# Two of six short convolutions move from VectorE to TensorE, as products with diagonal matrices

## The chip, the core and the metric

The kernel runs on one core of one Trainium2 chip. The metric is device time in microseconds (us). A time that is compared is a median over several runs; the profile is of one execution and has its own time.

## What is computed

A gated linear attention layer with a ternary feed-forward behind it, on 8 sequences of 256 tokens with 256 channels, all in float32. The part that matters here is the projection to q, k and v with a causal convolution over four tokens for each channel, and SiLU behind it:

```python
def causal_dwconv_silu(x, w):
    """Depthwise causal conv1d (kernel CONV) + SiLU. x: [B,T,C], w: [C,K]."""
    K = w.shape[1]
    xp = jnp.pad(x, ((0, 0), (K - 1, 0), (0, 0)))
    y = jax.lax.conv_general_dilated(jnp.transpose(xp, (0, 2, 1)), w[:, None, :], (1,), 'VALID', feature_group_count=w.shape[0])
    return jax.nn.silu(jnp.transpose(y, (0, 2, 1)))
...
q = causal_dwconv_silu(x @ Wq.T, conv_wq).reshape(B, T, H, DK)
k = causal_dwconv_silu(x @ Wk.T, conv_wk).reshape(B, T, H, DK)
v = causal_dwconv_silu(x @ Wv.T, conv_wv).reshape(B, T, H, DV)
beta = jax.nn.sigmoid(x @ Wb.T)
g = -jnp.exp(A_log) * jax.nn.softplus(x @ Wa.T + dt_bias)
...
def step(S, inp):
    qt, kt, vt, gt, bt = inp
    S = S * jnp.exp(gt)[..., None, None]
    v_new = vt - jnp.einsum('bhk,bhkv->bhv', kt, S)
    S = S + bt[..., None, None] * (kt[..., :, None] * v_new[..., None, :])
    o = jnp.einsum('bhk,bhkv->bhv', qt, S)
    return (S, o)
```

There are 6 heads, with 32 channels each for q and k and 64 for v: 768 projected channels, which are six groups of 128.

## The kernel before

The eight sequences are worked in four pairs of 512 tokens. For each pair a front part makes q, k, v and small matrices for each chunk of 32 tokens, and a recurrence then carries the state over the eight chunks. The program of each engine is written by hand in the order in which it is to run, and semaphores (`after(engine, semaphore, count, ...)`) hold the engines together; no scheduler moves anything.

A **prologue** makes the front of pair 0 and, for all pairs at once, the gates beta and g. Then come four **turns**. Turn k (function `turn` of each engine) runs the recurrence of pair k through chunks c = 0 to 7, and between its steps lies the front of pair k+1, in turns 0, 1 and 2, and the tail (output projection, layer norms, feed-forward) of pair k-1.

One chunk step goes round four engines. TensorE multiplies into the bank `pc` (`from_state`, `solve`), ScalarE copies the result to `u_sb` (`u_out`, L686), TensorE multiplies it into `pc` again and then into `po` (`to_state`), VectorE adds the state `s_sb` (`next_state`, L1085), and TensorE reads it for the next chunk; VectorE makes `r_sb` on the way (`residual`, L1073), and ScalarE copies `po` out (L693).

A group j of 128 projected channels passes through these steps:

- `project(k, j)`, L346: TensorE makes the group's projection in one half of the bank pair `pj`, half j mod 2, from two float32 products of 512 columns.
- `tile_out_of_psum(k, j)`: ScalarE copies it to `raw` (L623), a tile with three zero columns ahead of each sequence, and writes it, times the last tap, to the tile `conv`, which the profile calls `conv_buf` (L624).
- `conv_taps(k, j)`, L928: VectorE adds the other three taps, one instruction for each.
- `silu(k, j)`, L650: ScalarE takes SiLU into `kq` (groups 0 to 2) or `v_ch`, the tile named `x1_buf` in the program and `x_buf` in the profile (groups 3 to 5). Groups 2 and 5 take four instructions on 64 partitions each.

Behind the six groups, in chunks 3 and 4 of a turn, come `exponents` (L367, TensorE, into both halves of `pj`) with `exp_d` (L656, ScalarE), `square` (L664, ScalarE), `v_to_tokens` (L949, VectorE), `factors` (from L962, VectorE), and the matrices `dt_m` and `cm` on GpSimd (L849, L854).

In the prologue ScalarE's order is: the copies and SiLUs of all six groups, then `alog` (L802) and the softplus of the gates (L804 to L807), which waits for VectorE's preparation of `abt`. TensorE's order is: six projections, then 32 narrow products for the gates (L572), then a product that spreads the gates over the partitions (L579), which waits for VectorE.

## Time and profile before

| | us |
|---|---|
| median of 3 runs | 422.68 (421.88 to 423.92) |
| the profiled execution, its own time | 424.54 |
| its span, first to last instruction | 422.7 |
| VectorE busy | 315.2 (75%) |
| TensorE busy, products | 268.4 (63%) |
| ScalarE busy | 142.2 (34%) |
| GpSimd busy | 45.8 (11%) |
| mean granted TensorE clock | 0.766 of full |

No engine is busy all the time. The span is a chain that goes from engine to engine, so what counts is which work the chain passes through, and the order in which each engine takes its work. Times below are from the span's start. Turn 0 begins at about 82 us, turn 1 at about 158, turn 2 at about 250 and turn 3 at about 339.

### The profile page before, as it was taken

What the parts mean: (1) busy time and instruction counts of PE and PEld (TensorE: products, weight loads), DVE (VectorE), ACT (ScalarE), POOL (GpSimd) and SP (SyncE); (2) the same over time, 40 slices, a digit from 0 to 9 for tenths busy, and PEclk for the clock granted to TensorE, in tenths of its full rate; (3) what the DMA queues carried; (4) which work ended last, traced back from release to release, by engine and by line L of the source; (5) the groups of instructions that cost most, each with busy time, mean ns of one, the idle gap of its engine ahead of it and who ended that gap; (6) DMA issues with size and microseconds to landing.
All of it is one profiled execution on the core that took longest, in us unless ns stands there. A gap on an engine that the chain in (4) does not pass through costs nothing.

```text
span 422.7 us, 14141 instructions
## 1 busy us (share of the span) xinstructions
PE 268.4 (63%) x6314; PEld 181.3 (43%) x6314; DVE 315.2 (75%) x790; ACT 142.2 (34%) x341; POOL 45.8 (11%) x59
## 2 busy tenths in 40 slices
PE   3992710598576639797586559785666093986552
PEld 1481500545454417364554436454534072754431
DVE  0765998938698993949698996767989938248996
ACT  0874540047704610354523412357036000232010
POOL 1000240002520000012320000025200000000000
PEclk9965675589867867988666679897888567899665
DMA  8400000000000010000000020000000111000101
GB/s 255 181 0 2 2 0 0 5 2 3 4 3 2 4 50 3 2 3 2 3 4 2 3 99 3 2 4 2 5 2 2 51 51 53 3 3 14 40 0 50
DMA packets 8012, 9.70 MB, mean 23 GB/s; under 512 B 1808, under 2 KB 7056, under 8 KB 7952
## 3 DMA queue, kind: packets, MB, share of 16 engines
q1 hardware_dynamic: 7024, 8.41, 6.0%
q8 instruction: 49, 0.80, 0.8%
q10 hardware_dynamic: 928, 0.39, 0.4%
q14 instruction: 11, 0.09, 0.1%
HBM read 6.70 MB, written 2.10 MB: 21 GB/s over the span
## 4 chain that ended last, share of the span: by engine, by line
DVE 53%; PE 30%; issue 7%; ACT 6%; DMA 1%; DVEq 0%; SPq 0%; ACTq 0%
PE pc L333 7%; PE pj L346 6%; PE pg L457 4%; DVE sub_buf L1027 3%; DVE conv_buf L928 3%; DVE sub_buf L1025 3%; PE fr L572 2%; PE fr L480 2%; PE pj L457 2%; PE fr L333 2%; DVE chunk_buf L984 2%; DVE r_sb L1073 2%; DVE ss L962 2%; DVE r_all L916 1%; DVE t_all L915 1%
## 5 line engine op out<-in xcount | busy, mean ns | idle before, releaser
L928 DVE SCALAR_TENSOR_TENSOR conv_buf<-raw,wconv,conv_buf 128x512 f32<-128x512 f32 x72 | 55.5, 777 | 16.5 <-ACT conv_buf L624 14.8
L346 PE MATMUL pj<-xt,wproj 128*128 128x512 f32 x96 | 54.6, 705 | 8.2 <-DMA xt<-x_t 7.3
L686 ACT ACTIVATE u_sb<-pc 128x192 f32<-128x192 f32 x32 | 10.5, 329 | 116.3 <-PE pc L333 116.2
L876 POOL TENSOR_TENSOR s_dec<-s_sb,decay 128x192 f32<-128x192 f32 x24 | 14.5, 602 | 264.2 <-DVE s_sb L1082 169.6
L333 PE MATMUL pc<-r_sb,t_t 32*32 32x64 f32 x672 | 17.8, 244 | 35.2 <-DVE r_sb L1073 34.5
L333 PEld LDWEIGHTS pc<-r_sb,t_t 32*32 32x32 f32 x672 | 12.6, 120 | 46.0 <-DVE r_sb L1073 42.8
L333 PE MATMUL fr<-dt_m,chunk_buf 32*32 32x32 f32 x768 | 10.5, 219 | 34.3 <-DVE dt_m L1041 20.2
L346 PEld LDWEIGHTS pj<-xt,wproj 128*128 128x128 f32 x96 | 19.4, 221 | 26.9 <-issue 22.6
L358 PE MATMUL pg<-xt,wproj 128*128 128x512 f32 x48 | 29.6, 747 | 0.0
L457 PE MATMUL pg<-wout,conv_buf 128*128 128x256 f32 x36 | 15.2, 607 | 19.5 <-DVE conv_buf L1119 19.5
L333 PEld LDWEIGHTS fr<-dt_m,chunk_buf 32*32 32x32 f32 x768 | 9.7, 131 | 35.9 <-issue 35.9
L333 PE MATMUL pc<-u_sb,kg_tok 32*32 32x64 f32 x672 | 17.8, 246 | 11.3 <-ACT u_sb L686 11.3
L723 ACT ACTIVATE rv<-v_tok,bv 128x64 f32<-128x64 f32 x96 | 23.9, 338 | 0.0
L333 PEld LDWEIGHTS pc<-u_sb,kg_tok 32*32 32x32 f32 x672 | 12.7, 122 | 24.6 <-ACT u_sb L686 14.0
L693 ACT ACTIVATE o_all<-po 128x192 f32<-128x192 f32 x32 | 10.5, 329 | 33.8 <-PE po L333 33.7
L333 PE MATMUL pc<-s_sb,kc_ch 32*32 32x64 f32 x672 | 16.8, 236 | 7.8 <-DVE s_sb L1085 4.4
L457 PEld LDWEIGHTS pg<-wout,conv_buf 128*128 128x128 f32 x36 | 11.0, 315 | 24.8 <-DVE conv_buf L1119 22.4
L1085 DVE TENSOR_TENSOR s_sb<-s_dec,pc 128x192 f32<-128x192 f32 x24 | 8.4, 348 | 17.0 <-PE pc L333 16.8
L333 PE MATMUL po<-u_sb,a_t 32*32 32x64 f32 x768 | 19.3, 238 | 1.8 <-ACT u_sb L686 1.8
L333 PEld LDWEIGHTS pc<-s_sb,kc_ch 32*32 32x32 f32 x672 | 12.2, 116 | 17.0 <-issue 9.7
L333 PE MATMUL fr<-kq 32*32 32x64 f32 x768 | 19.0, 273 | 0.0
L333 PEld LDWEIGHTS fr<-kq 32*32 32x32 f32 x768 | 17.4, 146 | 1.2 <-issue 1.1
(161 smaller groups left out, 577.4 us busy)
## 6 DMA issues: line engine op xcount, KB each, us to landing
xt<-x_t SPq DMA_DIRECT2D x1, 1536.0 KB, 9.1
x_buf<-x SPq DMA_DIRECT2D x3, 512.0 KB, 3.8
out<-hid_buf SPq DMA_DIRECT2D x6, 256.0 KB, 2.2
wproj<-w_proj SPq DMA_DIRECT2D x1, 1024.0 KB, 8.1
xt<-x_t SPq DMA_DIRECT2D x1, 512.0 KB, 5.9
kq<-x SPq DMA_DIRECT2D x1, 512.0 KB, 3.7
out<-v_tok SPq DMA_DIRECT2D x2, 256.0 KB, 2.1
wout<-w_out SPq DMA_DIRECT2D x1, 384.0 KB, 9.5
```

Source lines behind the costliest of these rows:

```text
L333: mm = pe.matmul(out[rows], stationary[rows], moving[rows], **flags)
L346: mm = pe.matmul(pj[:, j % 2, :], wproj[:, t, j * P:(j + 1) * P], xt[:, t, k * TOK:(k + 1) * TOK], start=(t == 0), stop=(t == KT - 1))
L358: mm = pe.matmul(pg[:, :], wproj[:, t, w * P:(w + 1) * P], xt[:, t, k * TOK:(k + 1) * TOK], start=(t == 0), stop=(t == KT - 1))
L457: mm = pe.matmul(y_bank[part][:, (n % 2) * HID:(n % 2 + 1) * HID], o_ch[:, j, n * P:(n + 1) * P], wout[:, j, :], start=(j == 0), stop=(j = ...
L480: mm = pe.matmul(fr[:, n // 2, (n % 2) * HID:(n % 2 + 1) * HID], xq_t[:, n, t, :], wsplit[:, w, t, :], start=(t == 0 and w == 0), stop=(t ...
L686: act.activation(u_sb[:, :, :].rearrange("p g v -> p (g v)"), pc[:, 0:G3 * DV], ACT.Copy).then_inc(u_done, 1)
L693: act.activation(o_all[:, :, c, :], po[:, 0:G3 * DV].rearrange("p (g v) -> p g v", g=G3), ACT.Copy).then_inc(o_out, 1)
L723: e = act.activation(rv[:, k % 2, g, c, :], v_tok[:, g, c, :, :].rearrange("p h v -> p (h v)"), ACT.Identity, scale=bv[:, g * NC + c:g * N ...
L876: pool.tensor_tensor(s_dec[:, :, :], s_sb[:, :, :], decay[:, :, c:c + 1].to_broadcast([P, G3, DV]), ALU.mult).then_inc(sdec_done, 1)
L928: e = dve.scalar_tensor_tensor(out=conv[:, d, :, :], in0=raw[:, d, :, m:m + T], scalar=wconv[:, j, m:m + 1], in1=conv[:, d, :, :], op0=ALU ...
L1025: own(dve.tensor_tensor(step, inv16[:, j:j + 1, :, j + 1:HALF].to_broadcast(grid), inv16[:, 0:j, :, j:j + 1].to_broadcast(grid), ALU.mult))
L1027: own(dve.tensor_tensor(below, below, step, ALU.add))
```

## The change

Groups 4 and 5 (`BANK_TILES`) are no longer convolved by VectorE. At the start VectorE builds eight diagonal matrices `wdiag` of 128 x 128, one for each tap of each of the two groups. ScalarE copies the projection to `raw` as before but writes no `conv` tile for these groups. TensorE then multiplies the four shifted views of `raw` by the four diagonal matrices, float32 by float32 and 512 columns each, and adds them up in the same half of `pj` from which `raw` was copied (`conv_in_bank`). ScalarE takes SiLU straight from there.

```diff
+BANK_TILES = (4, 5)
+COPIED_TILES = CONV_TILES - len(BANK_TILES)
...
+        wdiag = sb("wdiag", [P, len(BANK_TILES), TAPS, P])
...
+            def conv_in_bank(k, j):
+
+                n = BANK_TILES.index(j)
+                if first(k):
+                    pe.wait_ge(diag_done, len(BANK_TILES) * TAPS)
+                after(pe, raw_in, n + 1, k, len(BANK_TILES))
+                for m in range(TAPS):
+                    mm = pe.matmul(pj[:, j % 2, :], wdiag[:, n, m, :], raw[:, SLOT[j], :, m:m + T],
+                                   start=(m == 0), stop=(m == TAPS - 1))
+                mm.then_inc(conv_mm, 1)
...
             def exponents(k):
 
                 after(pe, gm_done, 1, k, 1)
-                after(pe, tile_out, CONV_TILES, k, CONV_TILES)
+                after(pe, silu_done, CONV_TILES, k, CONV_TILES)
...
                     if front and c == 3:
-                        exponents(k + 1)
+                        conv_in_bank(k + 1, 4)
                     if front and c == 4:
                         chunk_products(k + 1, 0)
                     to_state(k, c)
+                    if front and c == 3:
+                        conv_in_bank(k + 1, 5)
+                    if front and c == 4:
+                        exponents(k + 1)
                     if front and c == 4:
                         chunk_products(k + 1, 1)
...
             mm.then_inc(ab_done, 1)
             pe.wait_ge(ld_const, 16)
+            for j in BANK_TILES:
+                conv_in_bank(0, j)
             pe.wait_ge(rep_in, 4)
...
-                act.activation(raw[:, SLOT[j], :, TAPS - 1:], bank, ACT.Copy)
+                moved = act.activation(raw[:, SLOT[j], :, TAPS - 1:], bank, ACT.Copy)
+                if j in BANK_TILES:
+                    moved.then_inc(raw_in, 1)
+                    return
...
             def silu(k, j):
-                after(act, conv_done[j], 1, k, 1)
+                if j in BANK_TILES:
+                    after(act, conv_mm, BANK_TILES.index(j) + 1, k, len(BANK_TILES))
+                    conved = pj[:, j % 2, :].rearrange("p (b t) -> p b t", b=2)
+                else:
+                    after(act, conv_done[j], 1, k, 1)
+                    conved = conv[:, SLOT[j], :, :]
...
-                    if front and c == 3:
-                        silu(k + 1, 4)
                     o_out_of_psum(k, c)
...
                     if front and c == 3:
+                        silu(k + 1, 4)
+                        silu(k + 1, 5)
+                    if front and c == 4:
                         exp_d(k + 1)
-                        silu(k + 1, 5)
...
-                    if front and c == 3:
-                        conv_taps(k + 1, 4)
...
-                    if front and c == 3:
-                        conv_taps(k + 1, 5)
...
             dve.wait_ge(ld_conv, 16)
-            for j in (0, 1):
-                conv_taps(0, j)
-            for j in range(2, CONV_TILES):
+            dve.wait_ge(ld_const, 16)
+            for n, j in enumerate(BANK_TILES):
+                for m in range(TAPS):
+                    dve.tensor_scalar(wdiag[:, n, m, :], cst[:, C_IDENT:C_IDENT + P], wconv[:, j, m:m + 1],
+                                      None, ALU.mult).then_inc(diag_done, 1)
+            for j in range(COPIED_TILES):
                 conv_taps(0, j)
```

Three places show what stands in a row on an engine before and now. Each row is an instruction or several equal ones, with the semaphores that it waits for. Lines of the changed program carry other numbers: L679 there is L650 here, L831 and L833 are L802 and L804, L715 is L686, L722 is L693, L685 is L656, L693 is L664, L337 is L333 and L382 is L367; L361 is `conv_in_bank`.

First ScalarE in the prologue, from the SiLU of group 3 to the first step of the softplus, before:

```order
L650 ACTIVATE x_buf<-conv_buf 128x2x256 [waits conv_done3]
L650 ACTIVATE x_buf<-conv_buf 128x2x256 [waits conv_done4]
L650 ACTIVATE x_buf<-conv_buf 64x256 [waits conv_done5]
L650 ACTIVATE x_buf<-conv_buf 64x256 x3
L802 ACT_TABLE_LOAD
L802 ACTIVATE alog<-alog 128x6 [waits ld_small]
L804 ACTIVATE abt<-abt 128x16x6 [waits abt_abs]
```

and after the change:

```order
L679 ACTIVATE x_buf<-conv_buf 128x2x256 [waits conv_done3]
L679 ACTIVATE x_buf<-pj 128x2x256 [waits conv_mm]
L679 ACTIVATE x_buf<-pj 64x256 [waits conv_mm]
L679 ACTIVATE x_buf<-pj 64x256 x3
L831 ACT_TABLE_LOAD
L831 ACTIVATE alog<-alog 128x6 [waits ld_small]
L833 ACTIVATE abt<-abt 128x16x6 [waits abt_abs]
```

The SiLUs of groups 4 and 5 keep their places ahead of `alog` and the softplus, and what they wait for is now TensorE's `conv_mm`.

Second TensorE in turn 0, from the solve of chunk 3 to the solve of chunk 4, before:

```order
L333 MATMUL pc<-r_sb,t_t 32x64 x11
L367 MATMUL pj<-gm,cst 128x384 [waits tile_out,gm_done]
L367 MATMUL pj<-gm,cst 128x384
L333 MATMUL pc<-u_sb,kg_tok 32x64 [waits u_done]
L333 MATMUL pc<-u_sb,kg_tok 32x64 x11
L333 MATMUL po<-u_sb,a_t 32x64 x12
L333 MATMUL pc<-s_sb,kc_ch 32x64 [waits s_done]
L333 MATMUL pc<-s_sb,kc_ch 32x64 x11
L333 MATMUL po<-s_sb,qe_ch 32x64 [waits o_out]
L333 MATMUL po<-s_sb,qe_ch 32x64 x11
L333 MATMUL pc<-r_sb,t_t 32x64 [waits r_done]
L333 MATMUL pc<-r_sb,t_t 32x64 x11
```

and after the change, as far as the products that open chunk 4:

```order
L337 MATMUL pc<-r_sb,t_t 32x64 x11
L361 MATMUL pj<-raw,wdiag 128x512 [waits raw_in]
L361 MATMUL pj<-raw,wdiag 128x512 x3
L337 MATMUL pc<-u_sb,kg_tok 32x64 [waits u_done]
L337 MATMUL pc<-u_sb,kg_tok 32x64 x11
L337 MATMUL po<-u_sb,a_t 32x64 x12
L361 MATMUL pj<-raw,wdiag 128x512 [waits raw_in]
L361 MATMUL pj<-raw,wdiag 128x512 x3
L337 MATMUL pc<-s_sb,kc_ch 32x64 [waits s_done]
L337 MATMUL pc<-s_sb,kc_ch 32x64 x11
L337 MATMUL po<-s_sb,qe_ch 32x64 [waits o_out]
L337 MATMUL po<-s_sb,qe_ch 32x64 x11
```

The convolution of group 4 stands between the solve of chunk 3 and its state product, that of group 5 between the state product and the start of chunk 4, and the exponents are no longer here: the diff has them behind the state product of chunk 4.

Third ScalarE in chunks 3 and 4 of turn 0, before:

```order
L686 ACTIVATE u_sb<-pc 128x192 [waits u_mm]
L650 ACTIVATE x_buf<-conv_buf 128x2x256 [waits v_tok_done,conv_done4]
L693 ACTIVATE o_all<-po 128x3x64 [waits o_mm]
L656 ACT_TABLE_LOAD
L656 ACTIVATE gm<-pj 128x384 [waits dexp_mm]
L656 ACTIVATE gm<-pj 128x384
L650 ACT_TABLE_LOAD [waits v_tok_done]
L650 ACTIVATE x_buf<-conv_buf 64x256 [waits conv_done5]
L650 ACTIVATE x_buf<-conv_buf 64x256 x3
L664 ACTIVATE gate_buf<-tok_buf 128x1536 [waits og_done,kq_tok_done]
L686 ACTIVATE u_sb<-pc 128x192 [waits u_mm]
L693 ACTIVATE o_all<-po 128x3x64 [waits o_mm]
```

and after the change:

```order
L715 ACTIVATE u_sb<-pc 128x192 [waits u_mm]
L722 ACTIVATE o_all<-po 128x3x64 [waits o_mm]
L679 ACTIVATE x_buf<-pj 128x2x256 [waits v_tok_done,conv_mm]
L679 ACTIVATE x_buf<-pj 64x256 [waits v_tok_done,conv_mm]
L679 ACTIVATE x_buf<-pj 64x256 x3
L693 ACTIVATE gate_buf<-tok_buf 128x1536 [waits og_done,kq_tok_done]
L715 ACTIVATE u_sb<-pc 128x192 [waits u_mm]
L722 ACTIVATE o_all<-po 128x3x64 [waits o_mm]
L685 ACT_TABLE_LOAD
L685 ACTIVATE gm<-pj 128x384 [waits dexp_mm]
L685 ACTIVATE gm<-pj 128x384
```

Both SiLUs now stand behind the copy of `po` in chunk 3, with the square and the `u_sb` copy of chunk 4 behind them; the exponentials and their table load stand behind chunk 4's copy of `po`, and the load that brought SiLU back is gone from here.

## Rows read from the trace of the kernel before

**Rows 1.** The page's chain that ended last: shares of the span by engine.

```profile
...
DVE 53%; PE 30%; issue 7%; ACT 6%; DMA 1%; DVEq 0%; SPq 0%; ACTq 0%
...
```

**Rows 2.** Groups by line: count, then busy us, mean ns, idle us before them.

```profile
...
L928 DVE SCALAR_TENSOR_TENSOR conv_buf<-raw,wconv,conv_buf 128x512 f32<-128x512 f32 x72 | 55.5, 777 | 16.5 <-ACT conv_buf L624 14.8
...
L624 ACT ACTIVATE conv_buf<-pj,wconv 128x512 f32<-128x512 f32 x24 | 16.5, 687 | 0.0
...
```

**Rows 3.** Timeline of ScalarE in the prologue: start, duration, engine, line, operation, [idle before].

```profile
...
26.95 1.69 ACT L650 ACTIVATE x_buf<-conv_buf 64x256 f32<-64x256 f32 x4 [0.96 <-DVE conv_buf L928]
28.66 1.28 ACT L802 ACT_TABLE_LOAD   x1
29.95 0.21 ACT L802 ACTIVATE alog<-alog 128x6 f32<-128x6 f32 x1
32.00 0.29 ACT L804 ACTIVATE abt<-abt 128x96 f32<-128x96 f32 x1 [1.84 <-DVE abt L1328]
...
```

**Rows 4.** Timeline of VectorE in the prologue.

```profile
...
13.40 13.52 DVE L928 SCALAR_TENSOR_TENSOR conv_buf<-raw,wconv,conv_buf 128x512 f32<-128x512 f32 x18 [13.40 <-ACT conv_buf L624]
30.78 0.36 DVE L1324 COPY ab<-fr 128x192 f32<-128x192 f32 x1 [3.86 <-PE fr L572]
...
```

**Rows 5.** Transfers: issuing queue, count, size, us to landing.

```profile
...
cst<-consts ACTq DMA_DIRECT2D x1, 371.5 KB, 6.0
...
```

**Rows 6.** Timeline of TensorE: float32 products at full clock, and bfloat16 ones.

```profile
...
13.33 7.13 PE L346 MATMUL pj<-xt,wproj 128*128 128x512 f32 x16 [0.91 <-ACT conv_buf L624]
...
95.01 1.98 PE L346 MATMUL pj<-xt,wproj 128*128 128x512 f32 x4
...
187.80 1.48 PE L480 MATMUL fr<-wsplit,tok_buf 128*128 128x256 bf16 x12
...
```

**Rows 7.** Chain of waits in order of time: four half-clock records.

```profile
...
85.73 3.44 PE pj L346 x4
...
```

**Rows 8.** Busy time by stretch; behind the fifth engine PEclk, the granted clock.

```profile
...
28.00:30.00 2.00, 2.00 (x11) 2.00 (x11) 0.00 (x0) 1.96 (x4) 0.00 (x0) 0.50 0.00 0
...
```

**Rows 9.** Timeline of TensorE in chunks 3 and 4, turns 0, 1 and 2.

```profile
...
104.75 1.56 PE L367 MATMUL pj<-gm,cst 128*128 128x384 f32 x4
...
114.48 0.86 PE L333 MATMUL pc<-u_sb,kg_tok 32*32 32x64 f32 x24 [2.92 <-ACT u_sb L686]
...
195.27 2.89 PE L367 MATMUL pj<-gm,cst 128*128 128x384 f32 x4
198.10 0.54 PE L333 MATMUL pc<-u_sb,kg_tok 32*32 32x64 f32 x24
198.46 0.51 PE L333 MATMUL po<-u_sb,a_t 32*32 32x64 f32 x24
...
285.15 1.56 PE L367 MATMUL pj<-gm,cst 128*128 128x384 f32 x4
...
```

**Rows 10.** Timeline of ScalarE in chunks 3 and 4, turns 0, 1 and 2.

```profile
...
111.00 1.69 ACT L650 ACTIVATE x_buf<-conv_buf 64x256 f32<-64x256 f32 x4
112.72 1.48 ACT L664 ACTIVATE gate_buf<-tok_buf 128x1536 f32<-128x1536 f32 x1
114.11 0.31 ACT L686 ACTIVATE u_sb<-pc 128x192 f32<-128x192 f32 x1
...
205.97 0.31 ACT L686 ACTIVATE u_sb<-pc 128x192 f32<-128x192 f32 x1
...
219.96 0.60 ACT L703 ACTIVATE gate_buf<-pg 128x512 f32<-128x512 f32 x1 [3.77 <-PE pg L358]
...
294.92 0.31 ACT L686 ACTIVATE u_sb<-pc 128x192 f32<-128x192 f32 x1
...
```

**Rows 11.** Timeline of VectorE in turns 0 and 1, behind the state of chunk 4.

```profile
...
115.68 1.74 DVE L962 TENSOR_REDUCE ss<-gate_buf 128x48 f32<-128x1536 f32 x1
...
218.24 0.96 DVE L999 STREAM_TRANSPOSE chunk_buf<-dt_m 128x768 f32<-128x768 f32 x1
...
```

**Rows 12.** Timeline of GpSimd in turn 1: the mask over the exponentials.

```profile
...
202.72 1.80 POOL L849 TENSOR_TENSOR dt_m<-gm,cst 128x768 f32<-128x768 f32 x1
...
```

More of the change, by code:

```diff
@@ L228, in program @@
         zeroed, vec_own, act_own, ffn_ready = (sem(n) for n in ("zeroed", "vec_own", "act_own", "ffn_ready"))
+        diag_done, raw_in, conv_mm = (sem(n) for n in ("diag_done", "raw_in", "conv_mm"))
         proj_done, tile_out, silu_done, kc_part, on_scaled = (
@@ L342, in project @@
                         after(pe, y_in, 0, k - 1, 2)
-                if not (first(k) and j < 2):
-                    after(pe, tile_out, j - 1, k, CONV_TILES)
+                if j >= 2:
+                    after(pe, tile_out, j - 1, k, COPIED_TILES)
                 for t in range(KT):
@@ L649, in silu @@
                     src = slice(0, 2) if b is None else b
-                    e = act.activation(dst, conv[rows, SLOT[j], src, :], ACT.Silu)
+                    e = act.activation(dst, conved[rows, src, :], ACT.Silu)
                 e.then_inc(silu_done, 1)
@@ L924, in conv_taps @@
             def conv_taps(k, j):
-                after(dve, tile_out, j + 1, k, CONV_TILES)
+                after(dve, tile_out, j + 1, k, COPIED_TILES)
                 for m in range(TAPS - 1):
```

## The prediction

> **What bounds the kernel now.** I read the page first, then the groups by line, then the chain of waits and the timelines of the two places that the change touches. The chain that ended last runs over VectorE for 53% of the span and over TensorE for 30% [rows 1], so VectorE instructions look like what it pays to remove, and the convolution's are the costliest group: 72 of 777 ns [rows 2]. But the diff takes only those of groups 4 and 5, at fixed places, so the question is which wait ends last at those places: once in the prologue, and in chunks 3 and 4 of turns 0, 1 and 2.
>
> In the prologue VectorE sits idle for 3.86 us behind the convolutions, until 30.78, when TensorE's gate products (L572) are done [rows 4]. ScalarE is idle for 1.84 us ahead of the softplus step L804, which starts at 32.00 [rows 3]. From there the path goes through softplus, gates and chunk matrices with no long idle time; the end of the six groups has slack and L804 has none.
>
> In chunks 3 and 4 the step that holds the recurrence is ScalarE's `u_sb` copy of chunk 4 (114.11, 205.97, 294.92). It stands straight behind the SiLU of group 5 and the square, and once it is done TensorE goes on after 2.92 us of idleness [rows 9, 10]. VectorE's reduction L962 follows at 115.68 [rows 11]; from there to the chunk matrices VectorE is nearly full, so a delay of this copy is passed on to the end.
>
> **The price of one convolution.** It is four float32 products of 512 columns, against two for a projection, so eight records of the kind of L346. Sixteen such records at full clock take 7.13 us and four take 1.98 us [rows 6]. Both fit r = 0.43 us a record plus 0.26 us at the end. At half clock four take 3.44 us [rows 7], 0.86 each. The next TensorE work starts 0.06 to 0.07 us before such a group's recorded end (195.27 + 2.89 against 198.10) [rows 9], ScalarE 0.04 after it. So a convolution at 2.4 GHz costs TensorE 8 x 0.43 + 0.19 = 3.63 us, and ScalarE may read it after 8 x 0.43 + 0.30 = 3.74 us. Reading through shifted views of `raw` and a diagonal stationary matrix have no row of their own; I take the projection's rate, since type, columns and partitions are the same. The lower bound is the bfloat16 row: 12 records of 256 columns in 1.48 us [rows 6], which is about 0.21 us for 512 columns, half of r.
>
> The Trainium skill ("TensorE: Matmul & The Clock Gate", section "Back-to-back issue gap") gives about 131 ns a pass for sustained streams of 512 columns, against 216 ns alone. By that a record of two passes would be 0.26 us instead of 0.43 and the whole change would come to about +3 us. The trace speaks for the slower figure: 16 records in a row keep 0.43 us [rows 6].
>
> **Prologue.** TensorE's two convolutions stand behind the gate products, so they start at 30.7. The granted clock there is 0.50 of full, that is 1.2 GHz [rows 8]: 32 narrow products have not kept it up. How many of the 16 records stay at half clock is not shown. Elsewhere four did (3.44 us) [rows 7], or the 2.83 us of the exponents from 195.27 before the rows turned short [rows 9]. I take four: 3.44 + 12 x 0.43 = 8.60 us, and 0.30 more until ScalarE starts the SiLU of group 5, at 39.60. All at full clock would be 6.88, all at half 13.76.
>
> ScalarE works in order, and both SiLUs stand ahead of `alog` and the softplus. Behind the SiLU of group 5 come its own 1.71 us (26.95 to 28.66), the table load to 29.95 (1.29), and `alog`, 0.23 [rows 3]. So L804 starts at 39.60 + 3.23 = 42.83 instead of 32.00: **+10.83 us**, 9.1 if all records run at full clock and 16.0 if none does. VectorE waits for the softplus and everything behind waits for VectorE; I find nothing later there that has been waiting for something else.
>
> The Trainium skill ("ScalarE: Activation LUTs", section "What ACT_TABLE_LOAD costs") adds a drain of about 1.38 us to each load. That would make it +12.2. The trace shows none: the load starts 0.02 us after the SiLU and `alog` 0.01 us after the load [rows 3].
>
> What VectorE loses there, 6 instructions of some 0.75 us, lies ahead of 3.86 us of idleness and gains nothing. The eight diagonals are built before 13.40, where VectorE has nothing else [rows 4]; the constants take 6.0 us to land [rows 5]. Even at 0.78 us each (a full convolution tap, four times as wide) they would end at about 13.5, so they cost nothing. ScalarE's two spared `conv` writes of 0.69 us [rows 2] gain nothing for the same reason.
>
> **Chunks 3 and 4 of a turn.** Let E be the start of the exponents today: 104.75, 195.27, 285.15 [rows 9]. The convolution of group 4 starts there instead, its `raw` being there since chunk 2. Then follow in TensorE's order the state product of chunk 3, 0.80 us (198.10 to 198.46 + 0.51, less the 0.07), and the convolution of group 5. ScalarE then does the SiLU of group 5 and the square, 3.11 us from its start to that of the `u_sb` copy (111.00 to 114.11) [rows 10]. Sum: 3.63 + 0.80 + 3.74 + 3.11 = 11.28 us behind E. In turn 1 the exponents ran at half clock, 2.89 us against 1.56; three records of the first convolution there are 0.43 us longer, +1.29.
>
> - turn 0: 104.75 + 11.28 = 116.03 against 114.11, +1.92
> - turn 1: 195.27 + 12.57 = 207.84 against 205.97, +1.87
> - turn 2: 285.15 + 11.28 = 296.43 against 294.92, +1.51
>
> TensorE has no long gap ahead of chunk 4's state product any more, so I take that at 0.54 us instead of 0.86 [rows 9] and subtract 0.32 from each: +1.60, +1.55, +1.19, **+4.3 us** together. Of what goes away (VectorE's six instructions, the exponents ahead of the state product, exponentials and table loads between two `u_sb` copies) all is counted, since E + 11.28 holds none of it.
>
> Moved work that is hidden: VectorE's layer-norm moments in chunk 3 now run while TensorE convolves. The exponents run behind chunk 4's state product, the exp load beside them, then the exponentials and GpSimd's mask, 1.80 us [rows 12]. In turn 1 that ends at about 215, and the matrices (L999, today 218.24) want it at about 220 [rows 11]. The SiLU table returns ahead of the gate's SiLU, where ScalarE is idle for 3.77 us [rows 10] against a load of 1.28. If that cover were gone each would cost its own length, at most 1.3 us a turn.
>
> **Sum.** 10.8 + 4.3 = +15.2 us. The profiled execution, 424.54, becomes 439.7; it lies 1.86 above the median, so the median 422.68 becomes **437.9 us**.
>
> **Rivals.**
>
> *Not slower, cheap products.* As a function of r the prologue gives 20r + 2.2 and the turns 51r - 17.6, together 71r - 15.4. It is zero at r = 0.216. If products with `raw` ran at the bfloat16 row's 0.213 us a record, the two convolutions would hide where VectorE's did and the time would be 422.4. Only the bfloat16 row speaks for it; every float32 row of 512 columns speaks against. Chance 0.03. A gain beyond 0.5% needs r under 0.19, which no row shows.
>
> *The turns break even.* The recurrence may get the 4.3 us back: at full clock the later solve and state products, as the one of 0.86 us [rows 9], would be 0.32 shorter, and two or three a turn lie on the path; a wait later in the turn may also end on something else. Then only the prologue counts: 422.68 + 10.8 = 433.5. For it: TensorE is busier. Against: VectorE is the fuller engine after 115.68 [rows 11]. Chance 0.14.
>
> *The clock stays low.* All 16 records of the prologue at half clock are +5.2, and one more first convolution of a turn at half clock is +3.4: 437.9 + 8.6 = 446.5. For it: rows at 0.50 in the prologue [rows 8]; against: dense work of this kind has brought the clock back in each row I read. Chance 0.11.
>
> **Chances and range.** Forecast 0.72. About 0.5%, some 2 us, is what a measurement of this kernel can tell from no change. Faster by more than that 0.01, within it 0.03, slower 0.96. The lower end takes the break-even turns and the prologue at full clock partly (9.1 + 1 is 432.8), the upper the prologue wholly at half clock (443.1): **432.5 to 443.5 us**.
>
> **What would show it.** In the changed profile: ScalarE idle for some 10 us ahead of the SiLU of group 4 in the prologue and some 3 us ahead of that of group 5, released by TensorE's L361; the `alog` table load at about 41.3; eight convolution records in 3.7 us in each turn; chunk 4's `u_sb` copy 11.3 us behind the first of them; VectorE idle in chunk 3 where its taps stood. I am wrong if L361's records are far from 0.43 us, if the softplus doesn't wait for them, or if the stretch from chunk 5 to the next turn changes its length by more than 1 us.

## The result

| | before | changed |
|---|---|---|
| median, us | 423.24 (421.88 to 423.92, 4 runs) | 441.91 (439.73 to 443.68, 4 runs) |
| the profiled execution, own time | 424.54 | 441.51 |
| its span | 422.7 | 439.7 |
| mean granted TensorE clock | 0.766 | 0.800 |

The changed kernel is slower: ratio (its time over that of before) 1.0443, 95% interval 1.0387 to 1.0499. The forecast was 437.9 us with a range of 432.5 to 443.5. The page of the changed kernel, busy times and the chain by engine:

```profile
PE 292.2 (66%) x6378; PEld 188.7 (43%) x6378; DVE 303.2 (69%) x774; ACT 136.5 (31%) x333; POOL 42.0 (10%) x59
...
DVE 49%; PE 37%; issue 6%; ACT 5%; DMA 1%; DVEq 0%; SPq 0%; ACTq 0%
```

VectorE was relieved of 12 us and TensorE was given 24, and the chain moved the same way: 37% over TensorE now, where [rows 1] had 30%. The groups by line (count, busy us, mean ns, idle us before them), where [rows 2] had 72 taps:

```profile
L957 DVE SCALAR_TENSOR_TENSOR conv_buf<-raw,wconv,conv_buf 128x512 f32<-128x512 f32 x48 | 36.6, 769 | 7.1 <-ACT conv_buf L648 6.0
L361 PE MATMUL pj<-raw,wdiag 128*128 128x512 f32 x64 | 31.9, 646 | 0.0
```

So 18.9 us of VectorE's taps became 31.9 us of TensorE's products. Line numbers have moved: L928 is L957 now, L650 is L679, L664 is L693, L686 is L715, L804 is L833, L849 is L878, L962 is L991.

**The prologue** of the changed kernel, TensorE (start, duration, engine, line, operation, [idle before]), then ScalarE. These answer to [rows 3, 6]:

```profile
27.80 2.50 PE L591 MATMUL fr<-wab,xt 128*128 128x12 f32 x11
30.14 9.71 PE L361 MATMUL pj<-raw,wdiag 128*128 128x512 f32 x16
```

```profile
36.46 0.60 ACT L679 ACTIVATE x_buf<-pj 128x512 f32<-128x512 f32 x1 [11.76 <-PE pj L361]
39.89 1.55 ACT L679 ACTIVATE x_buf<-pj 64x256 f32<-64x256 f32 x4 [2.84 <-PE pj L361]
41.46 1.28 ACT L831 ACT_TABLE_LOAD   x1
42.75 0.21 ACT L831 ACTIVATE alog<-alog 128x6 f32<-128x6 f32 x1
42.87 0.27 ACT L833 ACTIVATE abt<-abt 128x96 f32<-128x96 f32 x1
```

ScalarE does nothing for 11.76 and then 2.84 us, each time released by TensorE's L361, with the softplus step L833 behind it in its order. That step starts at 42.87; it was at 32.00.

**Chunks 3 and 4 of turn 0** of the changed kernel: TensorE, then ScalarE, against [rows 9, 10]:

```profile
116.03 3.70 PE L361 MATMUL pj<-raw,wdiag 128*128 128x512 f32 x8
119.67 0.54 PE L337 MATMUL pc<-u_sb,kg_tok 32*32 32x64 f32 x24
120.03 0.51 PE L337 MATMUL po<-u_sb,a_t 32*32 32x64 f32 x24
120.47 3.70 PE L361 MATMUL pj<-raw,wdiag 128*128 128x512 f32 x8
...
127.67 0.54 PE L337 MATMUL pc<-u_sb,kg_tok 32*32 32x64 f32 x24 [1.12 <-ACT u_sb L715]
```

```profile
120.83 0.59 ACT L679 ACTIVATE x_buf<-pj 128x512 f32<-128x512 f32 x1
124.21 1.55 ACT L679 ACTIVATE x_buf<-pj 64x256 f32<-64x256 f32 x4 [2.78 <-PE pj L361]
125.78 1.49 ACT L693 ACTIVATE gate_buf<-tok_buf 128x1536 f32<-128x1536 f32 x1
127.29 0.33 ACT L715 ACTIVATE u_sb<-pc 128x192 f32<-128x192 f32 x1
```

The `u_sb` copy of chunk 4 starts 127.29 - 116.03 = 11.26 us behind the first convolution. Eight records take 3.70 us and the next TensorE work starts 3.64 us in.

**Behind the reduction `ss`** come VectorE's small factors, with GpSimd's mask beside them, both of the changed kernel in turn 0.

```profile
130.97 0.18 DVE L943 TENSOR_TENSOR rt<-r 128x24 f32<-128x24 f32 x1
131.18 0.18 DVE L944 SCALAR_TENSOR_TENSOR rt<-rt,kk 128x24 f32<-128x24 f32 x1
131.40 1.67 DVE L945 SCALAR_TENSOR_TENSOR r<-rt,r 128x24 f32<-128x24 f32 x1
133.11 0.18 DVE L943 TENSOR_TENSOR rt<-r 128x24 f32<-128x24 f32 x1
```

```profile
131.20 1.83 POOL L878 TENSOR_TENSOR dt_m<-gm,cst 128x768 f32<-128x768 f32 x1 [8.27 <-ACT gm L685]
```

L945 on 24 elements a partition takes 0.18 us each time but one in a turn: when it starts 0.20 us behind the mask it is over at 133.07, 0.04 us after the mask's end. The same stands at 223.15 and 315.15. In the kernel before, the mask ran at 110.81 in turn 0, while VectorE had nothing to do.

**Where the 17.0 us of the two profiled executions lie.** The marks are VectorE's reduction `ss` (the first is the prologue's) and its reduction `m_o`, which opens the tail; the interval columns are differences of their starts in the two traces.

| interval | before | changed | difference | predicted |
|---|---|---|---|---|
| start to first `ss` | 45.89 | 56.97 | +11.08 | +10.83 |
| to `ss` in turn 0 | 69.79 | 71.58 | +1.79 | +1.60 |
| to `m_o` | 30.53 | 32.00 | +1.47 | 0 |
| to `ss` in turn 1 | 61.33 | 59.75 | -1.58 | +1.55 |
| to `m_o` | 30.53 | 31.71 | +1.18 | 0 |
| to `ss` in turn 2 | 58.42 | 60.29 | +1.87 | +1.19 |
| to `m_o` | 30.55 | 31.71 | +1.16 | 0 |
| to the end | 95.7 | 95.7 | 0.0 | 0 |

Prologue +11.1, convolutions in the turns +2.1, the stretches behind `ss` +3.8. The prediction named a change of more than 1 us from chunk 5 to the next turn as a sign of being wrong; that is the interval from `ss` to `m_o`, and it changed by 1.2 to 1.5 us in each turn.

### The profile page after: what moved, and what is told of

Read it like the earlier page. It is cut to its first block, busy times and chain, and to the rows that moved or that the text cites. A ratio compares the mean times of both kernels' runs of the same rounds, so it can differ in the third digit from the quotient of the medians.

```text
span 439.7 us, 14243 instructions
## 1 busy us (share of the span) xinstructions
PE 292.2 (66%) x6378; PEld 188.7 (43%) x6378; DVE 303.2 (69%) x774; ACT 136.5 (31%) x333; POOL 42.0 (10%) x59
## 2 busy tenths in 40 slices
DMA packets 8013, 9.71 MB, mean 22 GB/s; under 512 B 1808, under 2 KB 7056, under 8 KB 7952
## 4 chain that ended last, share of the span: by engine, by line
DVE 49%; PE 37%; issue 6%; ACT 5%; DMA 1%; DVEq 0%; SPq 0%; ACTq 0%
PE pc L337 8%; PE pj L361 7%; PE pj L350 6%; PE pg L472 3%; DVE sub_buf L1056 3%; DVE sub_buf L1054 3%; PE fr L337 3%; PE fr L591 2%; PE fr L495 2%; PE pj L472 2%; DVE r_sb L1102 2%; DVE conv_buf L957 2%; DVE ss L991 2%; DVE r L945 2%; PE po L337 1%
## 5 line engine op out<-in xcount | busy, mean ns | idle before, releaser
L715 ACT ACTIVATE u_sb<-pc 128x192 f32<-128x192 f32 x32 | 10.6, 331 | 111.3 <-PE pc L337 111.2
L957 DVE SCALAR_TENSOR_TENSOR conv_buf<-raw,wconv,conv_buf 128x512 f32<-128x512 f32 x48 | 36.6, 769 | 7.1 <-ACT conv_buf L648 6.0
L905 POOL TENSOR_TENSOR s_dec<-s_sb,decay 128x192 f32<-128x192 f32 x24 | 13.1, 547 | 266.2 <-DVE s_sb L1111 167.4
L337 PE MATMUL pc<-r_sb,t_t 32*32 32x64 f32 x672 | 17.3, 241 | 30.7 <-DVE r_sb L1102 29.4
L337 PE MATMUL fr<-dt_m,chunk_buf 32*32 32x32 f32 x768 | 12.0, 237 | 37.3 <-DVE dt_m L1070 20.0
L361 PE MATMUL pj<-raw,wdiag 128*128 128x512 f32 x64 | 31.9, 646 | 0.0
L337 PEld LDWEIGHTS pc<-r_sb,t_t 32*32 32x32 f32 x672 | 12.2, 118 | 41.2 <-DVE r_sb L1102 40.6
L337 PEld LDWEIGHTS fr<-dt_m,chunk_buf 32*32 32x32 f32 x768 | 11.2, 151 | 38.9 <-issue 38.9
L373 PE MATMUL pg<-xt,wproj 128*128 128x512 f32 x48 | 26.2, 671 | 0.0
L472 PE MATMUL pg<-wout,conv_buf 128*128 128x256 f32 x36 | 14.0, 565 | 18.0 <-DVE conv_buf L1148 18.0
L1102 DVE TENSOR_TENSOR r_sb<-pc,rv 128x192 f32<-128x192 f32 x28 | 9.9, 352 | 22.8 <-PE pc L337 22.4
L722 ACT ACTIVATE o_all<-po 128x192 f32<-128x192 f32 x32 | 10.5, 329 | 44.4 <-PE po L337 44.4
L337 PE MATMUL pc<-u_sb,kg_tok 32*32 32x64 f32 x672 | 17.3, 241 | 8.3 <-ACT u_sb L715 8.3
L337 PEld LDWEIGHTS pc<-u_sb,kg_tok 32*32 32x32 f32 x672 | 12.2, 118 | 21.1 <-ACT u_sb L715 10.9
L337 PE MATMUL po<-u_sb,a_t 32*32 32x64 f32 x768 | 19.4, 235 | 2.5 <-ACT u_sb L715 1.8
L337 PE MATMUL pc<-s_sb,kc_ch 32*32 32x64 f32 x672 | 16.6, 234 | 4.5 <-DVE s_sb L1114 2.0
L361 PEld LDWEIGHTS pj<-raw,wdiag 128*128 128x128 f32 x64 | 12.5, 204 | 14.3 <-issue 13.7
```

The source lines that it names most:

```text
L337: mm = pe.matmul(out[rows], stationary[rows], moving[rows], **flags)
L361: mm = pe.matmul(pj[:, j % 2, :], wdiag[:, n, m, :], raw[:, SLOT[j], :, m:m + T], start=(m == 0), stop=(m == TAPS - 1))
L373: mm = pe.matmul(pg[:, :], wproj[:, t, w * P:(w + 1) * P], xt[:, t, k * TOK:(k + 1) * TOK], start=(t == 0), stop=(t == KT - 1))
L472: mm = pe.matmul(y_bank[part][:, (n % 2) * HID:(n % 2 + 1) * HID], o_ch[:, j, n * P:(n + 1) * P], wout[:, j, :], start=(j == 0), stop=(j = ...
L715: act.activation(u_sb[:, :, :].rearrange("p g v -> p (g v)"), pc[:, 0:G3 * DV], ACT.Copy).then_inc(u_done, 1)
L905: pool.tensor_tensor(s_dec[:, :, :], s_sb[:, :, :], decay[:, :, c:c + 1].to_broadcast([P, G3, DV]), ALU.mult).then_inc(sdec_done, 1)
```

## The experiments

The theory was: the prologue costs some 10.8 us because the softplus stands behind the two SiLUs, the turns some 4 because two convolutions and the square stand in a row ahead of `u_sb`, and, as the trace of the changed kernel added, the mask costs VectorE 1.5 us a turn. The rivals: more products cost everywhere (a slower clock, a busier TensorE), or the parts hide behind each other.

The kernel before was measured again beside each set of runs, at 423.9, 424.5 and 424.2 us, so a difference of 1 us between runs of two sets says nothing.

### Softplus first

```diff
-            for j in range(CONV_TILES - CONV_DEPTH, CONV_TILES):
+            for j in range(CONV_TILES - CONV_DEPTH, COPIED_TILES):
                 silu(0, j)
...
             act.activation(abt[:, :, H:2 * H], ab[:, :, H:2 * H], ACT.Tanh, scale=0.5).then_inc(soft_done, 1)
+            for j in BANK_TILES:
+                silu(0, j)
```

> Only ScalarE's order in the prologue differs from the changed kernel: the softplus of the gates stands ahead of the SiLUs of groups 4 and 5. Theory (the prologue's price is the softplus queued behind the SiLUs that wait for TensorE): the softplus step starts near 32 us again instead of 42.87; TensorE's spreading product still can't start before the second convolution ends, at about 39.8 instead of 37.6, but then runs at full clock and is 1.3 shorter, so some 1 us stays: about 441.9 - 10.9 + 1 = 432. Rival (TensorE's own 9.7 us in the prologue are the price, whoever waits for them): no more than 2 us come back, 440 or more.

Measured: 434.02 us (432.93 to 436.33), ratio 1.0245 (1.0210 to 1.0281). The order of ScalarE alone gives 7.9 of the 18.7 us back. ScalarE in this run's prologue:

```profile
33.03 0.29 ACT L833 ACTIVATE abt<-abt 128x96 f32<-128x96 f32 x1 [6.94 <-DVE abt L1358]
...
41.39 1.54 ACT L679 ACTIVATE x_buf<-pj 64x256 f32<-64x256 f32 x4 [2.84 <-PE pj L361]
...
45.64 1.49 ACT L693 ACTIVATE gate_buf<-tok_buf 128x1536 f32<-128x1536 f32 x1
47.14 1.28 ACT L848 ACT_TABLE_LOAD   x1
```

The softplus is back at 33.03, released by VectorE as before. The first `ss` comes at 49.38, against 56.97 in the changed kernel and 45.89 before: it now stands behind the second convolution's SiLU (2.84 us of idleness), the copies and the square behind it, and a table load (L848) that only this order needs there. The expectation had counted 1 us for what stays. Of the 3.5 us that stay in this trace, 1.28 are the load, which I had overlooked; ScalarE's copies ahead of the square start 2.45 us later than before (42.96 against 40.51), behind that SiLU, so part of the convolutions' length stays on the path.

### The turns alone, and the prologue alone

For the first, pair 0 keeps VectorE's convolutions and the diagonals come in from turn 0 on:

```diff
+        def banked(k, j):
+            return k > 0 and j in BANK_TILES
...
-            for j in BANK_TILES:
-                conv_in_bank(0, j)
...
-            for j in range(COPIED_TILES):
+            for j in range(CONV_TILES):
                 conv_taps(0, j)
```

> Pair 0 is convolved by VectorE as before the change, pairs 1 to 3 by TensorE as in the changed kernel. If prologue and turns are separate prices, the prologue's 10.9 us go and what is left against before is the turns: 441.9 - 10.9 = 431.0, 7 to 8 us above before; by the sum of the prediction it would be 4.3 above before, 427.5. Rival (the prologue's delay hides part of the turns' cost or the other way): more than 2 us away from 431.

Measured: 431.67 us (430.84 to 433.72), ratio 1.0191 (1.0150 to 1.0233). The trace is of the slowest of the four runs, and 2.4 us of its excess lie ahead of the first `ss` (48.26 against 45.89), though pair 0 is convolved as before: the first projection started 0.9 us later, and the gate products took 11.26 us against 10.37 (granted clock 0.62 against 0.67). The intervals behind the first `ss` add up to +6.8 us. L949, which is L945 here, takes 1.67 us again, at 123.13.

For the second, only pair 0 has the diagonals, and the turns have the order of before:

```diff
+        def banked(k, j):
+            return k == 0 and j in BANK_TILES
...
                     if front and c == 3:
-                        conv_in_bank(k + 1, 4)
+                        exponents(k + 1)
...
-                    if front and c == 3:
-                        conv_in_bank(k + 1, 5)
-                    if front and c == 4:
-                        exponents(k + 1)
```

> The other half: only pair 0 is convolved by TensorE, and the turns are those of before. Theory: 423.2 + 10.9 = 434.1. Rival (later work absorbs part of the prologue's delay): under 432.

Measured: 435.08 us (434.66 to 435.32), ratio 1.0264 (1.0235 to 1.0293). The softplus starts at 42.22 and the first `ss` at 56.02. In its trace all intervals behind the first `ss` together are as before, within 0.1 us. The product of the two ratios is 1.0460; the whole change has 1.0443, well within its interval. So the parts add as far as can be measured. By the medians the 18.7 us are 11 in the prologue and 8 in the turns; by the traces the turns cost 6 to 7.

### Most of the mask left out

```diff
-                pool.tensor_tensor(dt_m[:, :, :], dexp[:, :, :], upper, ALU.mult).then_inc(dt_done, 1)
+                n = U if first(k) else 1
+                pool.tensor_tensor(dt_m[:, 0:n, :], dexp[:, 0:n, :], upper[:, 0:n, :], ALU.mult).then_inc(dt_done, 1)
```

> The changed kernel, with GpSimd's mask over the exponentials of pairs 1 to 3 reading one unit of 24 and leaving the others out. Theory (the mask now runs beside VectorE's factors and blocks a small instruction with two SBUF inputs for 1.5 us in each of three turns): that instruction is 0.18 us again, and the time falls by 4.5 us to about 437.4. Rival (the slow instruction comes from something else, such as waiting for its own result, or the gap closes on another wait): 441 or more.

Measured: 438.91 us (438.38 to 439.62), ratio 1.0356 (1.0325 to 1.0387). GpSimd's mask and VectorE's L946 (L945 of the changed kernel) in turn 0:

```profile
130.44 0.28 POOL L879 TENSOR_TENSOR dt_m<-gm,cst 128x32 f32<-128x32 f32 x1 [8.26 <-ACT gm L685]
130.64 0.18 DVE L946 SCALAR_TENSOR_TENSOR r<-rt,r 128x24 f32<-128x24 f32 x1
```

L946 is short again, and `ss` to `m_o` in turn 0 takes 30.05 us, less than the 30.53 of before. Of the 4.5 us that three such waits are, 3.0 came back in the median. By the two traces the stretches behind `ss` gave back 4.3 us, and those ahead of `ss` in turns 1 and 2 took 1.9 more: the output projection ran at a lower clock there, 5.22 and 5.49 us against 4.42 and 4.74 in the changed kernel. TensorE does just as much here as in the changed kernel, so a busier TensorE doesn't explain the stretch.

### The mask later

```diff
                 after(pool, dexp_done, 1, k, 1)
+                if not first(k):
+                    after(pool, c2_done, 1, k, 1)
                 pool.tensor_tensor(dt_m[:, :, :], dexp[:, :, :], upper, ALU.mult).then_inc(dt_done, 1)
```

> The changed kernel with GpSimd's mask (dt_m) of turns 0 to 2 held back until VectorE has made c2, so that it runs beside VectorE's scaled operands and no longer beside the small factor L945 (a two-operand instruction of 0.18 us that took 1.67 us in the changed kernel). Shared-port theory (a VectorE instruction that reads two operands from SBUF waits until the GpSimd mask is over): L945 returns to 0.18 us, and the wait moves with the mask to the first scaled operand L1015, which gets some 1.5 us longer; the time stays at 441.9, within 1.5 us. Rival (L945 is long for a reason of its own, for example because what it reads has just been written by ScalarE or TensorE is busier): L945 stays at 1.67 us wherever the mask is, and the time goes up by up to 1.5 us a turn.

Measured: 442.70 us (441.25 to 444.19), ratio 1.0425 (1.0399 to 1.0450): no difference from the changed kernel. VectorE, then GpSimd, in turn 0:

```profile
131.71 0.18 DVE L947 SCALAR_TENSOR_TENSOR r<-rt,r 128x24 f32<-128x24 f32 x1
...
134.15 1.71 DVE L1015 TENSOR_TENSOR chunk_buf<-tok_buf,nceg 128x256 f32<-128x256 f32 x1
135.78 1.70 DVE L1017 TENSOR_TENSOR sub_buf<-tok_buf,park 128x256 f32<-128x256 f32 x1
137.40 0.73 DVE L1015 TENSOR_TENSOR chunk_buf<-tok_buf,nceg 128x256 f32<-128x256 f32 x1
```

```profile
133.77 1.80 POOL L880 TENSOR_TENSOR dt_m<-gm,cst 128x768 f32<-128x768 f32 x1 [10.53 <-DVE c L1002]
135.66 1.54 POOL L885 TENSOR_TENSOR gm<-c,cst 128x768 f32<-128x768 f32 x1
```

The factor (L947 here) is at 0.18 us, and the wait has gone where the mask went: the first scaled operand waits for the mask, the second for the mask over `c` behind it (in the changed kernel they took 1.38 and 0.73). The wait belongs to two instructions that run at one time, not to L945. This decides against the rival.

### Two taps instead of four

```diff
-                for m in range(TAPS):
+                for m in range(2, TAPS):
                     mm = pe.matmul(pj[:, j % 2, :], wdiag[:, n, m, :], raw[:, SLOT[j], :, m:m + T],
-                                   start=(m == 0), stop=(m == TAPS - 1))
+                                   start=(m == 2), stop=(m == TAPS - 1))
```

> The changed kernel with only two of the four diagonal products for each of groups 4 and 5; the other two taps are left out, so its output isn't the reference's. It halves the one quantity r that both terms of the prediction hang on. If every record of L361 is on the path at 0.43 us: 8 records fewer in the prologue (3.44 us) and 8 fewer in each of three turns (10.3 us), 13.8 us in all: 441.9 becomes 428.1. Rival (something else ends last in the turns once the products are short, the square or VectorE): only the prologue's 3.4 and part of the turns' come back, 434 or more.

Measured: 429.43 us (425.57 to 429.68), ratio 1.0097 (1.0059 to 1.0134): 12.5 us less than the changed kernel, 13.8 expected; the spans differ by 13.9 (439.7 against 425.8). By the traces the first `ss` came 3.3 us earlier (53.64), and each interval that ends at `ss` in a turn was 3.6 us shorter (67.96 against 71.58 in turn 0), the rest unchanged within 0.3. Eight records of 0.43 us are 3.44. So the records that were left out had lain on the path in all four places, at their full length; no second wait lies right behind.

### The square earlier

```diff
-                    if front and c == 4:
-                        square(k + 1)
...
                         silu(k + 1, 4)
+                        square(k + 1)
                         silu(k + 1, 5)
```

> The changed kernel with the square put ahead of the SiLU of group 5 on ScalarE, where ScalarE waits 2.8 us for TensorE's second convolution; 1.4 us of work leave the stretch between that convolution and the u_sb copy of chunk 4. Theory: the u_sb copy of chunk 4 starts 1.1 to 1.5 us earlier in turns 0 to 2, but VectorE's transpose of v, which waits for the SiLU of group 5, and the reduction behind it then bound the turn, so only some 0.7 us a turn reach the end: about 439.9. Rival (the u_sb copy alone carries the path): 1.4 us a turn, 437.7. Rival (the path lies on VectorE wholly): 441.9.

Measured: 439.02 us (437.48 to 439.55), ratio 1.0332 (1.0312 to 1.0352), 2.9 us less. ScalarE in turn 0, where the convolutions start at 115.80:

```profile
121.08 1.49 ACT L693 ACTIVATE gate_buf<-tok_buf 128x1536 f32<-128x1536 f32 x1
123.98 1.55 ACT L679 ACTIVATE x_buf<-pj 64x256 f32<-64x256 f32 x4 [1.41 <-PE pj L361]
125.55 0.33 ACT L715 ACTIVATE u_sb<-pc 128x192 f32<-128x192 f32 x1
```

`u_sb` stands 9.75 us behind the first convolution, 1.51 less, but `ss` only 11.76 behind it, 0.76 less: VectorE's transpose of `v_tok`, which starts with the `u_sb` copy and lasts 1.84 us, comes ahead of it. Half of the gain goes there, as the theory had it. The medians can't tell the theory (2.0 us) from the rival (4.2): they differ by 2.9 us, and the two ratios by 4.7. The traces can: `ss` gained 0.76, 0.33 and 0.76 us on the first convolution in the three turns, and the whole span 2.0 (437.7 against 439.7).

The wait beside the mask is still there, but in turns 0 and 2 it is another instruction's:

```profile
129.75 1.73 DVE L939 TENSOR_SCALAR r<-rt 128x24 int32<-128x24 int32 x1
```

```profile
129.65 1.80 POOL L877 TENSOR_TENSOR dt_m<-gm,cst 128x768 f32<-128x768 f32 x1 [6.94 <-ACT gm L685]
```

L939 reads one tile, not two, and elsewhere takes 0.18 us. So "two operands from SBUF", as the shared-port theory puts it, doesn't cover every instruction that waits.

### The other mask later, in the kernel before

The same kind of wait was already in the kernel before: its mask over `c` (L854) stands beside L984 and L986. This holds it back until `kc` is made, and moves nothing else:

```diff
                 after(pool, c2_done, 1, k, 1)
+                if not first(k):
+                    after(pool, kc_done, 1, k, 1)
                 pool.tensor_tensor(cm[:, :, :], units(c2[:, :]), lower, ALU.mult).then_inc(cm_done, 1)
...
                         d_masked(k + 1)
+                    if front and c == 5:
                         c_masked(k + 1)
```

> The kernel before with only one of the two moves of the run that gave 418.4: GpSimd's mask cm held back until VectorE has made kc. Shared-port theory: L984 takes 0.41 us instead of 1.38 and L986 0.41 instead of 0.73 in each of turns 0 to 2, 1.3 us a turn on the path: 424.5 becomes 420.6, and the square has the other 2.2 us. Rival (the whole gain came from the square): 424.

Measured: 418.71 us (417.00 to 420.92) beside 424.20 for the kernel before, ratio 0.9874 (0.9839 to 0.9910). The kernel before, turn 0, VectorE and GpSimd:

```profile
120.97 1.38 DVE L984 TENSOR_TENSOR chunk_buf<-tok_buf,nceg 128x256 f32<-128x256 f32 x1
122.27 0.73 DVE L986 TENSOR_TENSOR sub_buf<-tok_buf,park 128x256 f32<-128x256 f32 x1
```

```profile
120.59 1.48 POOL L854 TENSOR_TENSOR gm<-c,cst 128x768 f32<-128x768 f32 x1 [7.97 <-DVE c L971]
```

and with the mask later (lines moved by 3):

```profile
121.09 0.41 DVE L987 TENSOR_TENSOR chunk_buf<-tok_buf,nceg 128x256 f32<-128x256 f32 x1
121.42 0.42 DVE L989 TENSOR_TENSOR sub_buf<-tok_buf,park 128x256 f32<-128x256 f32 x1
...
124.12 0.94 DVE L996 STREAM_TRANSPOSE qe_ch<-sub_buf 128x768 f32<-128x768 f32 x1
```

```profile
124.36 1.48 POOL L856 TENSOR_TENSOR gm<-c,cst 128x768 f32<-128x768 f32 x1 [7.90 <-DVE kc_ch L994]
```

From `ss` to the transpose into `kc_ch` it is 7.43 us instead of 8.70, as expected; `ss` to `m_o` is shorter by 1.59, 1.91 and 1.92 us. The 0.3 beyond the 1.3 in turn 0 is idleness ahead of the next state (1.02 us before `s_sb` has become 0.68). The mask now runs beside the transpose L996, which takes 0.94 us as it did before without a mask beside it (125.28, L993): it did not wait.

With the square moved ahead of the copy of `po` as well:

```diff
                         silu(k + 1, 4)
+                        square(k + 1)
                     o_out_of_psum(k, c)
```

> The kernel before, not the changed one, with two moves that the study's traces point to: the square of ScalarE ahead of the copy of po and the exponentials of chunk 3 instead of ahead of the u_sb copy of chunk 4, and GpSimd's mask cm held back until VectorE has made kc, so that it does not stand beside VectorE's two-operand instructions L984 and L986. Shared-port theory: L984 and L986 lose the 1.3 us a turn that they wait (-3.9), the square 0.8 us a turn (-2.4): 423.4 becomes 417 to 418. Rival (the waits hide behind something else): 422 to 423.5.

Measured: 418.38 us (416.60 to 420.68) beside 424.46, ratio 0.9852 (0.9827 to 0.9877). It is the fastest kernel of the study, faster than both that the case began with. The two intervals overlap, so the square's share, expected at 2.4 us, can't be told from nothing. Counted from the first `ss`, `u_sb` came 0.3 us earlier in turn 0 (113.24 - 45.30 against 114.11 - 45.89) and `ss` 0.2 later (69.95 against 69.79), for the same transpose is in the way. The mask has the gain, and I had expected it at 3.9 us where it is 5.5.

### All three in the changed kernel

Softplus first, the square early and the mask over `c` late, by the edits above.

> The changed kernel with everything that the study found to give back: the SiLUs of groups 4 and 5 of pair 0 behind the gates' softplus (gave 7.9 us alone), the square ahead of the SiLU of group 5 (gave 2.9 alone), and GpSimd's mask cm held back until VectorE has made kc, away from L1013 and L1015. If the shares add: 441.9 less 7.9, 2.9 and 3.9 is 427.2. That still lies some 9 us above the kernel before with its two moves (418.4), which is the price of the convolutions on TensorE in the turns and of the L945 wait. Rival (the three moves overlap on one wait): 430 or more.

Measured: 429.40 us (427.00 to 431.35) beside 424.20, ratio 1.0113 (1.0078 to 1.0148). By the traces the stretch behind `ss` is shorter by 1.5, 1.4 and 1.3 us. It is 2.2 us above the expected 427.2. The profiled execution was the slowest of the six (431.35), and in it 1.4 us of the excess show in turn 2, TensorE:

```profile
289.77 0.74 PE L337 MATMUL pc<-r_sb,t_t 32*32 32x64 f32 x24 [0.78 <-DVE r_sb L1106]
...
290.44 5.14 PE L361 MATMUL pj<-raw,wdiag 128*128 128x512 f32 x8
...
296.32 3.70 PE L361 MATMUL pj<-raw,wdiag 128*128 128x512 f32 x8
```

The same eight records take 5.14 and 3.70 us. Busy times of 290.40 to 292.40, PEclk behind the fifth engine, show 1.2 GHz:

```profile
290.40:292.40 2.00, 2.00 (x8) 0.92 (x4) 1.18 (x7) 0.33 (x1) 0.00 (x0) 0.50 0.00 0
```

So even mended, the convolutions on TensorE cost 429.4 - 418.4 = 11 us against the kernel before with the same mask move and a like move of the square. The waits beside the mask over the exponentials are among them (in turn 0 one of 1.73 us where 0.18 is usual), and so is the prologue's first `ss`, 4.4 us later (49.74 against 45.30).

## Why the prediction came out as it did

**The price of a convolution: right.** 3.70 us for eight records, 3.64 until TensorE's next work and 3.74 until ScalarE's SiLU (120.47 to 124.21), against a forecast of 3.70, 3.63 and 3.74. Shifted views of `raw` and a diagonal stationary matrix cost what the projection's operands cost. Halving the number of products showed that each record is paid in full. The rival of cheap products is out.

The Trainium skill ("TensorE: Matmul & The Clock Gate", section "Back-to-back issue gap") gives two rates for a matmul of 512 columns. As an estimate for a record, twice its 216 ns for an isolated one is what these records show (0.43 us); twice its 131 ns for a sustained stream would have made eight records 2.1 us, where the trace has 3.70.

**The prologue: the mechanism right, the close number by errors that cancel.** L833 at 42.87, forecast 42.83. The products started 0.56 us earlier than I said (30.14). They took 9.71 us where the forecast comes to 8.86 (8.60 and the 0.26 at the end), because the clock stayed low longer: by these lengths about six records at half clock, not four. From the SiLU of group 5 to L833 it was 2.98 us, not 3.23. That is -0.56 + 0.85 - 0.25. Busy times of the changed kernel by stretch, PEclk behind the fifth engine:

```profile
32.00:34.00 2.00, 2.00 (x4) 0.97 (x3) 1.28 (x1) 0.00 (x0) 0.00 (x0) 0.50 0.00 0
34.00:36.00 2.00, 2.00 (x4) 0.73 (x4) 0.00 (x0) 0.00 (x0) 0.00 (x0) 0.65 0.00 0
36.00:38.00 2.00, 2.00 (x6) 0.79 (x6) 0.00 (x0) 0.60 (x1) 0.00 (x0) 1.00 0.00 0
```

That the order of ScalarE makes it a cost was shown by putting the softplus first. L831's table load starts 0.02 us after the SiLU (39.89 + 1.55 to 41.46). The eight diagonals cost nothing, as forecast: VectorE built them in 1.66 us from 7.49 and was then idle for 4.56 us.

The Trainium skill ("ScalarE: Activation LUTs", section "What ACT_TABLE_LOAD costs") would have a drain of 1.38 us beside that load; the trace has none.

**The convolutions in the turns: the mechanism right, the size half.** 11.26 us from the first record to `u_sb` in each of the three turns, forecast 11.28. Of +4.3 us only +2.1 came, and the difference is the clock of TensorE at other places than I had put it. In turn 1 the 1.29 us for records at half clock did not come (3.70 us at 207.78). The output projection earlier in that turn ran at a better clock, 4.42 us against 5.49 before, and so did a group's projection between it and the convolutions, 2.69 us (194.30) against 3.38 (180.59). In turn 2 it went the other way: the output projection took 4.74 us against 4.27 and the projection behind it 2.85 (286.14) against 2.60 (271.75), which is the 0.7 us by which that turn lies above its forecast. The 1.29 us were real but not where I put them. In the run with the softplus first the convolution of turn 1 took 5.04 us, in the mended changed kernel that of turn 2 took 5.14. The price belongs into the range, at no fixed place.

**"Moved work that is hidden": wrong.** This is the step of the prediction that failed. I moved GpSimd's mask to about 131 in turn 0 and asked only when its result is wanted. The result was early enough. What I left out is what VectorE does in those 1.8 us, and whether the two can run together. Those instructions can't: 1.49 us a turn in L945, 3.8 us in the three intervals behind `ss`. Leaving most of the mask out, and moving it, showed that the overlap is the cause.

The Trainium skill ("SBUF — State Buffer", section "Who interferes with whom") has the rule: a VectorE instruction with two SBUF inputs contends with a GpSimd instruction that reads SBUF, and whoever comes first keeps the shared ports for its whole length. The trace agrees, 1.67 us instead of 0.18 beside a mask of 1.83. The runs show when instructions wait, not which port they wait for.

**The sum.** Against the forecast of +15.2 us the spans moved by +17.0: +0.25 in the prologue, -2.3 for the convolutions in the turns, +3.8 for the mask. The remaining 2.2 us of the 4.0 by which 437.9 was too low are no mechanism: the median of before with its fourth run is 0.56 higher, and the profiled execution of before lay 1.30 above that median, that of the changed kernel 0.40 below its own. A range built on one profiled execution can't be tighter than that. That the forecast came this close is partly luck: a cost of 3.8 us that I had put at nothing met a gain of 2.3 us by the clock that I had not foreseen either.

**The rivals.** Break-even turns are out: with the turns alone changed the kernel took 431.67 us, some 8 above before. Of the rival of a low clock only a part came: about two records more than forecast in the prologue, and none in the turns' convolutions of the changed kernel's trace.

**What stays open.** Why the clock falls in one turn and not in another isn't settled. The rows ahead of both look alike: short 32x64 products with idle times of 0.76 and 0.78 us. Nor does any run show why L939, with one input, waits where a transpose does not. What the change would cost with a mask that is out of VectorE's way altogether was not tried with the output kept.

## What to carry to other kernels

An edit that moves work on a lightly used engine is not free because its result comes early: look at what the neighbour does in that very stretch, and in the trace for one instruction that takes several times its siblings' time. Relieving the engine with the largest share of the chain gained nothing here, since the work went to the engine whose results the chain waits for next. A wait put ahead of an in-order engine's other work can cost nearly its full length, even when what waits is wanted late: moving the softplus ahead of two waiting SiLUs gave 7.9 us.

## What the runs showed of the hardware that I had not expected

- Some instructions of VectorE and GpSimd hold each other up, in both directions. VectorE's L945 took 1.67 us instead of 0.18, L984 1.38 instead of 0.41, and in the run with the square early the one-input L939 1.73 instead of 0.18. The transpose L996 beside a mask took its usual 0.94. GpSimd's three products for `kg_tok` took 2.65 us beside VectorE's taps in the kernel before, and 1.76 in the changed kernel, where VectorE is idle at that time:

```profile
108.19 2.65 POOL L861 TENSOR_TENSOR kg_tok<-tok_buf,park 128x256 f32<-128x256 f32 x3
```

```profile
121.17 1.76 POOL L890 TENSOR_TENSOR kg_tok<-tok_buf,park 128x256 f32<-128x256 f32 x3
```

- A mask that ran 1.48 us at the wrong place cost the kernel before 5.5 us of 424 over three turns, more than its three waits of 1.3 us.
- The clock of TensorE comes and goes at different places in kernels whose program is the same there: eight equal records took 3.70, 5.04 or 5.14 us.
